# Graph attention on one core: x loaded apart from the node table, and the residual add moved from VectorE to GpSimd

## What is computed

```python
messages = x[dst]
g = (messages @ W_gate.T + b_gate)[:, 0]
h = messages @ W_lin.T + b_lin
e = exp(g - segment_max(g, src)[src])
attn = e / (segment_sum(e, src) + 1e-16)[src]
pooled = segment_sum(attn[:, None] * h, src)
out = layernorm(x + pooled @ W_out.T + b_out)
```

## Time and profile before

| | us |
|---|---|
| median of 3 runs | 2803.58 (2803.17 to 2806.08) |
| profiled execution, its own time | 2809.35 |
| its span, first to last instruction | 2807.4 |
| busy in the span: POOL / DVE / PE | 1717.9 / 1682.9 / 956.4 |
| granted TensorE clock, mean | 0.601 of full |

### The profile page before, as it was taken

One profiled execution on the slowest core, in us unless ns is written; L12 is line 12 of the kernel. 1 busy time (PEld: TensorE's weight loads), 2 busy tenths in 40 slices (PEclk: granted clock), 3 DMA queues, 4 the chain that ended last, 5 costly groups with the idle time before them and its releaser, 6 DMA issues.

```text
span 2807.4 us, 24834 instructions
## 1 busy us (share of the span) xinstructions
PE 956.4 (34%) x4932; PEld 809.7 (29%) x4932; DVE 1682.9 (60%) x5593; ACT 147.1 (5%) x489; POOL 1717.9 (61%) x1781
## 2 busy tenths in 40 slices
PE   3522211224334342342433424434333242432250
PEld 3521110223233232332332423323233242332240
DVE  8699998546456465564654645546455464554377
ACT  0411110000000000000000000000000000000005
POOL 0010002777777777777777777777777777777723
PEclk9855555556555566555655656556566565565565
DMA  3130001222222222222222222222222222222652
GB/s 114 63 115 0 0 0 42 53 54 54 54 54 55 53 54 55 53 54 55 54 54 54 54 55 53 55 54 53 55 54 55 53 54 55 53 55 54 45 24 92
DMA packets 91888, 148.65 MB, mean 53 GB/s; under 512 B 30537, under 2 KB 62113, under 8 KB 91731
## 3 DMA queue, kind: packets, MB, share of 16 engines
q0 software_dynamic: 56224, 117.06, 21.8%
q1 hardware_dynamic: 34767, 31.04, 3.6%
q10 hardware_dynamic: 864, 0.20, 0.0%
HBM read 134.35 MB, written 13.83 MB: 53 GB/s over the span
## 4 chain that ended last, share of the span: by engine, by line
POOL 39%; DVE 24%; issue 22%; PE 6%; DVEq 3%; DMA 3%; another core or an unknown queue 1%; ACT 1%; ACTq 0%; POOLq 0%; SPq 0%
POOL arena L350 39%; DVE spread L867 4%; DVE nodes_sb L873 3%; PE bank L566 3%; DMA arena<-node_table,gather_at 3%; DVE rows_a L702 2%; DVE rows_a L701 2%; DVE rows_b L702 2%; DVE rows_b L701 2%; DVEq L895 1%; DVE turn_b L702 1%; PE bank L481 1%; DVE turn_b L701 1%; DVE turn_a L702 1%
## 5 line engine op out<-in xcount | busy, mean ns | idle before, releaser
L350 POOL DMA_INDIRECT arena<-node_table,gather_at x1757 | 1681.7, 957 | 829.7 <-issue 529.3
L566 PE MATMUL bank<-arena,spread 128*128 128x129 f32 x3520 | 750.7, 384 | 315.0 <-DVE nodes_sb L873 211.7
L566 PEld LDWEIGHTS bank<-arena,spread 128*128 128x128 f32 x3520 | 654.9, 280 | 405.9 <-DVE nodes_sb L873 285.1
L867 DVE TENSOR_SCALAR spread<-iota_row,place_t,weights 128x128 f32<-128x128 f32 x1760 | 600.9, 358 | 174.2 <-PE bank L566 74.5
L873 DVE SCALAR_TENSOR_TENSOR nodes_sb<-nodes_sb,weights,bank 128x129 f32 x1760 | 606.3, 345 | 56.4 <-PE bank L566 11.7
L845 DVE TENSOR_TENSOR_SCAN run_max<-pen,bank 40x128 f32<-40x128 f32 (+1 forms) x45 | 18.5, 412 | 744.3 <-PE bank L548 744.3
L548 PE MATMUL bank<-ident,arena 128*40 128x128 f32 (+1 forms) x45 | 17.1, 380 | 695.8 <-DMA arena<-node_table,gather_at 695.8
L548 PEld LDWEIGHTS bank<-ident,arena 128*40 128x40 f32 (+1 forms) x45 | 5.3, 118 | 703.8 <-issue 703.8
L345 POOL COPY nodes_sb<-blank_row 128x12642 f32<-128x12642 f32 x1 | 10.8, 10814 | 161.7 <-DMA node_table<-nodes_sb 161.7
L535 PE MATMUL bank<-ident,dst_f 40*128 40x40 f32 x44 | 13.1, 297 | 264.9 <-DVEq L676 264.9
L535 PEld LDWEIGHTS bank<-ident,dst_f 40*128 40x128 f32 x44 | 7.9, 179 | 275.1 <-issue 275.1
(11 more groups left out here) (151 smaller groups left out, 975.0 us busy)
## 6 DMA issues: line engine op xcount, KB each, us to landing
arena<-node_table,gather_at POOLq DMA_INDIRECT x1757, 22.6
node_table<-nodes_sb SPq DMA_DIRECT2D x1, 6347.7 KB
nodes_sb<-in_x SPq DMA_DIRECT2D x1, 6250.0 KB
arena<-in_x SPq DMA_DIRECT2D x12, 448.0 KB
out<-arena SPq DMA_DIRECT2D x12, 448.0 KB
k<-sorted_keys SPq DMA_DIRECT2D x132, 20.0 KB
turn_a<-in_src SPq DMA_DIRECT2D x1, 828.0 KB
turn_b<-in_dst SPq DMA_DIRECT2D x1, 828.0 KB
```

The costliest lines, as they stand in the source:

```text
L350: pool.indirect_dma_start(out=gathered_rows[par][:, t, :], out_offset=None, in_=table[:, :], in_offset=bass.IndirectOffsetOnAxis(ap=gather ...
L566: last = pe.matmul(tile_ps(slot), lhsT=spread[:, slot, :], rhs=gathered_rows[par][:, b * BATCH + u, 0:WIDTH], start=True, stop=True)
L867: return dve.tensor_scalar(spread[:, slot, :], iota_row[:, :], place_t[par][:, t:t + 1], weights[par][:, 0, t:t + 1], ALU.is_equal, ALU.mult)
```

## The change

`x` gets a tile of its own: `node_x`, 100 columns of 128 features with no gaps, in `nodes_sb` (which shrinks from 13000 to 12800 columns), loaded by four DMAs of 25 columns each with a semaphore each. `turn_nodes` waits for a quarter in the batch that first touches it. `node_rows` moves to `arena`, where the one-hot tiles lay. So POOL's memset of the ones (L341) waits for `hist_ready`, and the 12 loads of `x` into `arena` wait for `table_stored`. `COUNT_AT` becomes 13. In the output stage POOL does both the multiplication and the addition, and DVE waits for `resid_ready` instead of adding. SP's wait for `table_stored` at the very end goes away, since it has waited for it earlier.

```diff
-COUNT_AT = 12
+COUNT_AT = 13
+X_PARTS = 4
-        nodes_sb = sb("nodes_sb", [P, 13000])
-        node_rows = nodes_sb[0:NODE_ROWS, 0:NODE_COLS * ROW].rearrange("p (n f) -> p n f", f=ROW)
+        nodes_sb = sb("nodes_sb", [P, NODE_COLS * FEAT])
+        node_x = nodes_sb[0:NODE_ROWS, 0:NODE_COLS * FEAT].rearrange("p (n f) -> p n f", f=FEAT)
+        node_rows = arena[0:NODE_ROWS, 0:NODE_COLS * ROW].rearrange("p (n f) -> p n f", f=ROW)
...
-            sp.dma_start(node_rows[:, :, 1:1 + FEAT], x.rearrange("(p n) f -> p n f", n=NODE_COLS)).then_inc(x_loaded, 16)
+            for q in range(X_PARTS):
+                cols = slice(q * NODE_COLS // X_PARTS, (q + 1) * NODE_COLS // X_PARTS)
+                sp.dma_start(node_x[:, cols, :], x.rearrange("(p n) f -> p n f", n=NODE_COLS)[:, cols, :]).then_inc(x_loaded[q], 16)
...
-            sp.wait_ge(hist_ready, 1)
+            sp.wait_ge(table_stored, 16)
             for g in range(GROUPS - 2):
                 load_x(g)
...
             sp.wait_ge(stored, 16 * (GROUPS + 1))
-            sp.wait_ge(table_stored, 16)
...
+            pool.wait_ge(hist_ready, 1)
             pool.memset(node_rows[:, :, 0:1], 1.0).then_inc(ones_ready, 1)
...
                                    ALU.mult).then_inc(pooled_ready, 1)
+                pool.wait_ge(pooled_ready, g + 1)
+                pool.tensor_tensor(mixed[g % Z], mixed[g % Z], x_at[g], ALU.add).then_inc(resid_ready, 1)
...
+                for q in range(X_PARTS):
+                    if at <= q * NODE_COLS // X_PARTS < at + n:
+                        pe.wait_ge(x_loaded[q], 16)
-                    last = pe.transpose(bank[b % 2][:, c * NODE_ROWS:(c + 1) * NODE_ROWS], node_rows[:, at + c, 1:1 + FEAT],
+                    last = pe.transpose(bank[b % 2][:, c * NODE_ROWS:(c + 1) * NODE_ROWS], node_x[:, at + c, :],
...
-            pe.wait_ge(x_loaded, 16)
...
-            def add_x(g):
-                dve.wait_ge(pooled_ready, g + 1)
-                dve.tensor_tensor(mixed[g % Z], mixed[g % Z], x_at[g], ALU.add)
-                dve.drain()
...
             for g in range(GROUPS):
-                add_x(g)
+                dve.wait_ge(resid_ready, g + 1)
                 if g > 0:
                     scale_and_shift(g - 1)
                 measure(g)
```

More of the change, by code:

```diff
@@ L200, in tile_ps @@
             return bank[slot // 2][:, (slot % 2) * 256:(slot % 2) * 256 + WIDTH]
-        src_loaded, dst_loaded, x_loaded, weights_loaded = sem("src_loaded"), sem("dst_loaded"), sem("x_loaded"), sem("weights_loaded")
+        src_loaded, dst_loaded, x_loaded, weights_loaded = sem("src_loaded"), sem("dst_loaded"), [sem(f"x_loaded{q}") for q in range(X_PARTS)], sem("weights_loaded")
         iotas_ready, consts_ready = sem("iotas_ready"), sem("consts_ready")
@@ L223, in graph_attention @@
         x_in = sem("x_in")
-        dens_ready, pooled_ready = sem("dens_ready"), sem("pooled_ready")
+        dens_ready, pooled_ready, resid_ready = sem("dens_ready"), sem("pooled_ready"), sem("resid_ready")
         var_ready, std_ready, norm_ready, out_ready = sem("var_ready"), sem("std_ready"), sem("norm_ready"), sem("out_ready")
```

## The result

| | before | after |
|---|---|---|
| median of 4 runs | 2803.94 us (2803.17 to 2806.08) | 2773.91 us (2773.83 to 2774.84) |
| span of the profiled execution | 2807.4 us | 2773.0 us |
| its own time | 2809.35 us | 2774.84 us |
| first gather starts | 468.69 us | 445.53 us |
| last gather starts | 2684.8 us | 2660.8 us |

The ratio of the times is 0.9893, with a 95% interval of 0.9878 to 0.9909. The forecast was 2772 us in a range of 2766 to 2784; the kernel is 1.9 us above it.

A forecast was written before the change was run, and what follows sets the result against it. VectorE was taken to bound the sort and output stage, with a hole before the counts; GpSimd's gathers, 79% of the span, stay unchanged. Start 23.9 plus output stage 7.6 gives 31.5 us: 2803.6 to 2772, range 2766 to 2784.

The forecast's parts named there:

- The hole before the counts: At the start, VectorE's 24.9 us wait for the counts' matmul nearly goes, all reaching the first gather: 23.9 us gained.
- the first batches: First two node-table batches, 5.0 us after an idle PE, start quicker behind busy matmuls: gain 23.9, not 23.8.
- The load behind the histogram: Quarters of x land before PE asks, even at 92 GB/s, the last by some 2 us: load hidden.
- the load comes late: Rival at the start: first quarters of x come late and VectorE's hole stays; 2796 us or no change; 4%.
- The clock: PE's granted clock stays 1.00 (2.4 GHz) through the node batches, at 0.985 us each.
- The hold at the clearing: In the sort, GpSimd's clearing of the sums holds VectorE some 10.5 us, paid again, no more and no less.
- The output stage: GpSimd takes VectorE's 14 additions and sets the pace, 3.65 us a group for 4.30: 7.6 us gained.
- the shift's hold: In the output stage, VectorE's two-input shift waits for GpSimd, then holds its next instruction 0.2 us each group.
- The price of the rival: Output-stage rival: GpSimd's addition costs 2.1 to 2.45 us, output gain -2 to 4, total 2776 to 2782 us; 17%.
- part 2: The output-stage half of the change, additions moved from VectorE to GpSimd: 7.6 us gained.
- The upper bound: GpSimd's addition in the output stage costs at most 1.68 + 0.77 = 2.45 us, if the multiplication's repeated input were free.
- the slower rival: Moved tiles and table slow the 1757 gathers; 18 ns each decides, 25 ns more gives 2816 us; 3%.

The follow-up runs named there:

- e1: The changed kernel with only the new start, VectorE adding x in the output stage as before: 2778.67 us, ratio 0.9912.
- e3: The changed kernel with the counts' matmul one batch earlier (COUNT_AT 12 in place of 13): 2771.49 us, ratio 0.9886.
- e5: The changed kernel with x still in four loads, but in rows 130 columns apart, so pieces of 512 bytes: 3780.62 us, ratio 0.9922, on a slower chip.
- e4: The changed kernel with x loaded by one contiguous DMA in place of four: 3811.64 us, ratio 1.0003, on a slower chip.
- e7: The changed kernel with ScalarE clearing the sums in 33 small pieces in place of GpSimd's copy: 3770.07 us, ratio 0.9891, on a slower chip.
- e2: The kernel before with only the new output stage, GpSimd multiplying and adding: 2796.93 us, ratio 0.9977.
- e8: The changed kernel with every third output group adding the scales in place of x, and every third keeping its product in the sums: 2771.33 us.
- e9: The changed kernel with both operations of output group 0 on VectorE, the other groups on GpSimd: 2770.76 us, ratio 0.9885.

## Why the prediction was right, step by step

**The hole before the counts.** Right in mechanism and size: 23.9 us forecast, 23.2 at the first gather and 24.6 by e1. All its marks are there: PE's turn at 51.3, no wait for x, the table's store at 88.95, the first gather at 445.5. Two small things were off. PE's turn began 0.5 us later than forecast. And I took 0.1 us for the first batches, because they would start quicker behind busy matmuls: here they took 5.1 us to 56.4, as after an idle PE, the next took 1.36 and not 0.98, and the counts came 16.2 and not 15.7 us after the start. In other runs of the same order the counts came 15.2 us after it, so this part scatters by 1 us, and the 0.1 has nothing under it. By e3 that is worth at most 1 us.

**The load behind the histogram.** The bound was the old rate, 92 GB/s, with the last quarter 2 us ahead of its use. In the change it ran at 132 to 139 GB/s and was over before 57 us. e5 shows that the bound held too: at 92 GB/s until 76 us there is no wait. What the prediction did not ask is what else is on these engines. PE's first matmul waited 21.3 us for the bias and 16.2 before. VectorE's own work (the wait for it, 5.28 us, is in the timeline above) still came after it, so this cost nothing; the histogram began at 28.6 us, and in all runs but e4 between 27.7 and 28.6. e4, where the bias costs 31 us, shows how much hung on it. The rival "the load comes late" had the right place and the wrong transfer: not x is late but what stands beside it.

**The clock.** Right: 1.00 in 51.0 to 90.9 us, and a batch still takes 0.98 us.

**The hold at the clearing.** Right: 10.4 us paid again (10.98 less 0.55), and e7 shows that it was on the path.

**The output stage.** Right in mechanism, with the size 1.5 us too high: 7.6 forecast, 6.1 by the traces and 6.4 by e2. The mis-sized term is GpSimd's addition, 1.7 forecast and 2.07 us measured. It alone would make 13 x 0.37 = 4.8 us, but of the period only 0.14 (3.79 for 3.65) was lost: the 0.2 that I gave each period for the shift's hold was not there. GpSimd's instructions follow one another within 0.1 us and take 1.68 and 2.07 us whether a shift waits or not; how the shift slips between them was not looked for. That is 13 x 0.14 = 1.8 us. The first aggregate ends 0.3 later than forecast. The 1.7 that I gave once for a hold were 1.1: the second group came 1.7 late, but the last came 0.7 early, since its shift met no GpSimd instruction. Together 1.8 + 0.3 - 0.6 = 1.5, as measured. So the size came out as near as it did by luck: two terms were wrong in opposite directions, the addition by 0.37 us a group and the hold by 0.2. The price of the rival was off too. By the prediction's own terms an addition of 2.1 to 2.45 us makes periods of 4.05 to 4.4 us and a part 2 of about 2 to -3 us, not 4 to -2. The addition measured, 2.07, lies just under that rival's range, and part 2 gave 6.

The choice of 1.7 leant on the clearing copy: a multiplication costs twice a copy's price for an element, and "so seems to pay for its second stream". e8 shows that this holds only in part: the repeated input costs less than a full one, by 0.39 us for 896 elements. The upper bound, made on the other assumption, had the right sign and was twice as far off (0.77 for 0.39). The estimate from the Trainium skill ("GPSIMD Engine Reference", section 3.1) was 1.97 us for the addition, and the runs show 1.90 to 2.07: for the instruction it was nearer than my choice. The 4 us that it would have made of part 2 was not (6.1 to 6.4). Section 4.1 of the same page of the Trainium skill, by which elementwise work belongs on VectorE, is against this part; VectorE is the faster by 1.09 to 2.07 us, but it was the engine with no time left.

**Who meets whom.** The shift was held to 0.85 us in most groups and 1.34 in the first, and the seven measuring instructions with their one input (L942) took 1.45 us beside a busy GpSimd, as before. The Trainium skill's "SBUF — State Buffer", section "Who interferes with whom", says so: VectorE's second input comes through what it shares with GpSimd's reads, and one input does not meet it. The trace agrees with both halves.

**The gathers.** 1.261 us each on both sides; nothing of the slower rival came.

## What to carry to other kernels

When a load is moved off the path, list every other transfer that flies at the same time and what waits for it: here a 64 KB bias, and not the 6.4 MB, decided between 30 us gained and none. Look also at what a shared semaphore makes an engine wait for beyond what it reads. Moving an operation to a slower engine can pay when the faster one sets the pace and the slower has room. Here splitting it between VectorE and GpSimd by turns lost, as each waited for the other's instructions; only the first group, for which VectorE had stood idle, was worth keeping there (e9). A clearing that the mostly idle ScalarE did in small pieces cost nothing, where one long GpSimd copy stopped VectorE for its whole length.

## What the runs showed of the hardware that was not expected

- A 64 KB load on ScalarE's queue landed 12.9 us after its issue beside a load in pieces of 512 bytes, 17.6 to 19.0 beside four loads in pieces of 12.8 KB, and 53.8 beside pieces of 51.2 KB. With four loads in pieces of 512 bytes it was 9.4.
- GpSimd, 128 x 896 float32, two inputs: 1.68 us when the second repeats one number 128 times, 2.07 with a full one or a repeated row, 1.90 to 1.95 when the first comes from the sums. Addition or multiplication made no difference.
- On one chip the stretch from the first gather to the last took 993 to 996 us longer in all four profiles, with VectorE idle for up to 20 us at a time and GpSimd 42 times for some 24 us, waiting for ScalarE's word. The stretch before it and the output stage were unchanged. No run looked for the cause, and it stays open.
